# Cell builder of a graph network: PE's encode and transposes change places

## The reference

```python
# L1: a network that makes a 32x32 matrix for every edge, six message passes
eh  = relu(e_feat @ en1_w.T + en1_b)             # 200,000 x 128: built once, in the cell builder
w_e = (eh @ en2_w.T + en2_b).reshape(-1, D, D)
for _ in range(6):
    msg = einsum('ei,eio->eo', out[src], w_e)
    agg = segment_sum(msg, dst, num_segments=n_nodes) + conv_bias
    h   = gru_cell(relu(agg), h, ...)
# L0, L2, L3: out = segment_sum(weight[e] * x[src[e]], dst[e]), with different weights
```

## Time and profile before

| what | value |
|---|---|
| time, median of 3 runs | 24,022.46 us |
| lowest and highest run | 24,014.54 and 24,035.85 us |
| the profiled execution, its span | 30,532.6 us |
| the cell builder in it | 5,141 us, from 3,385 to 8,526 |
| DVE, POOL, PE, ACT busy in the cell builder | 3,460, 3,032, 2,962, 2,566 us |
| granted TensorE clock in the cell builder | 0.87 |

### The profile page before, as it was taken

The page is one execution under the profiler, slowest core; times in us unless marked ns, Lnnn a source line. Parts: engine busy times, 40 slices in busy tenths (PEclk is TensorE's granted clock), DMA queues, the critical chain, the costliest instruction groups (busy, mean ns, idle before and its releaser), DMA issues. The chain is left out here.

```text
span 30532.6 us, 420576 instructions
## 1 busy us (share of the span) xinstructions
PE 18622.1 (61%) x121575; PEld 13266.8 (43%) x121575; DVE 11720.7 (38%) x29589; ACT 7911.3 (26%) x20853; POOL 14020.9 (46%) x16639
## 2 busy tenths in 40 slices
PE   3333555555655676667666766676666766676654
PEld 3333322222244454455444554455445544554444
DVE  5444566666710333233323333233323332333220
ACT  0000344445510222222222322232222222232210
POOL 4886355555610444534453445344443445344520
PEclk5555788888977777777777877787777777787777
DMA  3222233322278222112211221122112221122147
GB/s 97 48 49 69 85 122 118 113 99 93 68 293 344 66 64 59 52 58 65 58 54 53 68 63 55 48 69 63 56 53 60 63 59 54 57 65 60 55 142 308
DMA packets 1398480, 2692.30 MB, mean 88 GB/s; under 512 B 938471, under 2 KB 1104704, under 8 KB 1189106
## 3 DMA queue, kind: packets, MB, share of 16 engines
q10 hardware_dynamic: 335568, 1445.71, 13.4%
q1 hardware_dynamic: 709952, 1053.68, 10.0%
q0 software_dynamic: 352256, 186.21, 4.3%
HBM read 2105.10 MB, written 1242.55 MB: 110 GB/s over the span
## 5 line engine op out<-in xcount | busy, mean ns | idle before, releaser
L785 POOL DMA_INDIRECT sb_xg<-node_rows,sb_src_c x9408 | 8876.9, 944 | 11917.8 <-SPq L803 6579.1
L921 PE MATMUL banks<-sb_work,sb_eh_sb 128*128 128x256 f32 x29184 | 8833.9, 453 | 1693.7 <-issue 1358.2
L921 PEld LDWEIGHTS banks<-sb_work,sb_eh_sb 128*128 128x128 f32 x29184 | 6472.3, 229 | 3674.0 <-issue 2259.6
L874 DVE TENSOR_TENSOR sb_work<-sb_xs,banks_p 128x2048 f32<-128x2048 f32 x1824 | 4171.1, 2288 | 9843.7 <-remote 5895.0
L978 ACT ACTIVATE sb_work<-banks 128x512 f32<-128x512 f32 x7296 | 4124.9, 599 | 11185.0 <-remote 7003.8
L1200 PE MATMUL banks<-sb_hot_code,sb_xs 128*128 128x392 bf16 x7296 | 1874.5, 371 | 2173.7 <-DVE sb_work L1163 1435.1
L1163 DVE SCALAR_TENSOR_TENSOR sb_work<-sb_work,sb_eh_sb,banks 128x784 f32 x2432 | 2502.3, 1029 | 572.4 <-PE banks L1202 484.1
L864 DVE COPY sb_xs<-sb_xg 128x32 f32 x14592 | 1762.7, 191 | 2459.9 <-issue 2268.6
L907 PE MATMUL banks_p<-sb_work,sb_en 128*32 128x256 f32 x29184 | 2084.7, 391 | 778.6 <-issue 766.1
L367 POOL DMA_INDIRECT slots<-sb_rows,sb_slot_u x1600 | 2108.6, 1318 | 786.7 <-issue 762.6
L1079 POOL TENSOR_SCALAR sb_xs<-sb_codes,sb_code 128x128 bf16<-128x128 f16 x2432 | 1516.6, 624 | 2067.3 <-PE banks L1202 2067.1
(11 more groups left out here) (281 smaller groups left out, 13084.1 us busy)
## 6 DMA issues: line engine op xcount, KB each, us to landing
sb_eh_sb<-eh ACTq DMA_DIRECT2D x912, 1024.0 KB
weights_between<-sb_work ACTq DMA_DIRECT2D x305, 1568.0 KB
edges_between<-sb_work ACTq DMA_DIRECT2D x305, 1568.0 KB
sb_work<-weights_between SPq DMA_DIRECT2D x147, 3136.0 KB, 12.5
sb_work<-edges_between SPq DMA_DIRECT2D x98, 3136.0 KB, 12.4
eh<-sb_eh_sb ACTq DMA_DIRECT2D x304, 512.0 KB, 2.6
sb_xg<-node_rows,sb_src_c POOLq DMA_INDIRECT x9408
sb_win_row<-window_rows SPq DMA_DIRECT2D x100, 488.3 KB
```

The source lines that it names most:

```text
L785: nc.gpsimd.indirect_dma_start(m.xg_ring[:, row % RING * D:(row % RING + 1) * D], None, m.node_dram, bass.IndirectOffsetOnAxis(ap=m.src_c[ ...
L874: V.tensor_tensor(m.spread[q], m.xs[h].rearrange("s (t i) -> s t i", i=D)[:, tiles, :].unsqueeze(3) .broadcast_to([P, TS, D, WN]), m.mask_ ...
L921: o = mm(m.ps_pair[u % 4][:, v, :, :], m.eh[h % 2][:, t * K:(t + 1) * K], m.spread[t // TS][:, t % TS, :, :], start=True, stop=True)
```

## The change

All in `build_cells`. In half c the engines now run:

- PE: tiles 0 and 1, encode of c, tiles 2 to 4, transposes of c+1, tiles 5 to 7.
- ACT: row operations of tiles 0 to 3, ReLU and DMA of c-1, tiles 4 and 5, copy of c+1, tiles 6 and 7, flush.
- DVE: adds 0 to 6, bias of c (its own half), add 7.

The first half's transposes and copy stand ahead of the loop, and on PE and ACT the last body is written out as well, since the last half has no successor to transpose.

```diff
+            keep_turned(0, 0, True)
+            for i, n, h in batches(act, behind=1):
                 for q in range(2):
                     c = n * 2 + q
-                    act.wait_ge(turned, c + 1)
-                    if not first(i, h):
-                        act.wait_ge(encoded, c - 1)
-                    nc.scalar.activation(m.attr_t[q], m.ps_turn[q], ACT.Copy).then_inc(turned_sb, 1)
                     for t in range(q * TS, q * TS + TS):
...
                         r.then_inc(weighted, 1)
+                        if t % TS == 3 and not (first(i, h) and q == 0):
+                            rectify(c - 1)
+                        if t % TS == 5 and not (isinstance(c, int) and c == last):
+                            keep_turned(c + 1, 1 - q, first(i, h) and q == 0)
                     if not (first(i, h) and q == 0):
-                        rectify(c - 1)
                         flush(i, c, 2 * h + q)
...
                     add(t)
-                    if t % TS == TS // 2 and not (first(i, h) and q == 0):
-                        bias(n * 2 + q - 1, first(i, h) and q == 1)
-            bias(2 * BATCHES - 1, False)
+                    if t % TS == 6:
+                        bias(n * 2 + q, first(i, h) and q == 0)
...
+                        if t % TS == 1:
+                            encode(c, q, first(i, h) and q == 0)
+                        if t % TS == 4 and not (isinstance(c, int) and c == last):
+                            turn_rows(c + 1, 1 - q, n + 1 + q, first(i, h) and q == 0)
```

More of the change, by code:

```diff
@@ L1030, in build_cells, with batches @@
         slots_v = m.slots.rearrange("(s t) r -> s t r", t=TP)
-        def batches(eng):
-            for i in peeled(eng, BODIES):
+        last = 2 * BATCHES - 1
+        def batches(eng, behind=0):
+            for i in peeled(eng, BODIES, behind=behind):
                 for h in range(L):
@@ L1101, in rectify, with keep_turned @@
                 act.dma_start(m.eh_dram[:, bass.ds(c * EC * K, EC * K)], m.eh_now).then_inc(eh_out, 16)
-            for i, n, h in batches(act):
+            def keep_turned(c, q, early):
+                act.wait_ge(turned, c + 1)
+                if not early:
+                    act.wait_ge(encoded, c - 1)
+                nc.scalar.activation(m.attr_t[q], m.ps_turn[q], ACT.Copy).then_inc(turned_sb, 1)
+            keep_turned(0, 0, True)
+            for i, n, h in batches(act, behind=1):
                 for q in range(2):
                     c = n * 2 + q
-                    act.wait_ge(turned, c + 1)
-                    if not first(i, h):
-                        act.wait_ge(encoded, c - 1)
-                    nc.scalar.activation(m.attr_t[q], m.ps_turn[q], ACT.Copy).then_inc(turned_sb, 1)
                     for t in range(q * TS, q * TS + TS):
@@ L1118, in _ @@
                         r.then_inc(weighted, 1)
+                        if t % TS == 3 and not (first(i, h) and q == 0):
+                            rectify(c - 1)
+                        if t % TS == 5 and not (isinstance(c, int) and c == last):
+                            keep_turned(c + 1, 1 - q, first(i, h) and q == 0)
                     if not (first(i, h) and q == 0):
-                        rectify(c - 1)
                         flush(i, c, 2 * h + q)
-            rectify(2 * BATCHES - 1)
+            rectify(last)
             flush(BODIES, 2 * BATCHES, 0)
@@ L1182, in _, with turn_rows, encode @@
             mm = nc.tensor.matmul
-            for i, n, h in batches(pe):
+            def turn_rows(c, q, loads, early):
+                pe.wait_ge(rows_in[q], loads * 16)
+                if not early:
+                    pe.wait_ge(turned_sb, c - 1)
+                for g in range(2):
+                    mt = nc.tensor.transpose(m.ps_turn[q][:, g * P:(g + 1) * P], m.attr[q][:, g * P:(g + 1) * P],
+                                             m.ident[:, :])
+                mt.then_inc(turned, 1)
+            def encode(c, q, early):
+                pe.wait_ge(turned_sb, c + 1)
+                if not early:
+                    pe.wait_ge(biased, c)
+                for g in range(2):
+                    me = mm(m.ps_encoded[:, g, :], m.attr_t[q][:, g * P:(g + 1) * P], m.en1[:, :], start=True, stop=True)
+                me.then_inc(encoded, 1)
+            turn_rows(0, 0, 1, True)
+            for i, n, h in batches(pe, behind=1):
                 for q in range(2):
                     c = n * 2 + q
[L1186 to L1192, removed]
                     for t in range(q * TS, q * TS + TS):
```

## The result

The changed kernel takes 23,474.44 us (median of 4 runs, 23,472.86 to 23,476.29), against 24,026.48 for the kernel before (4 runs): ratio 0.9772, 95% interval 0.9758 to 0.9786, 552 us less. The forecast was 23,780; the direction and the range held, the saving is 2.3 times the forecast's 240.

A forecast was written before the change was run, and what follows sets the result against it. A circle of waits (flush behind ReLU, ReLU behind bias, next rows behind flush) was taken to bound the cell builder. Periods over all halves summed to 4,879 us against 5,148, 269 saved, 240 timed: 23,780, range 23,430 to 24,050.

The forecast's parts named there:

- 18.6 + d: Forecast length in us of a half whose flush has data, from add 0 to the next add 0; before, 21.18.
- d: Delay of add 2 by the encode between PE's tiles 1 and 2: 1.7 us, between 0.74 and 3.5; 0.6 behind a flush.
- The conversion: Profile savings count 0.79 to 1 in timed runs, the profiled span being 27% longer: 269 us taken as 240.
- The circle of no-flush even halves: Add 2, transposes, copy, two tiles, flush step and next add 0 in series: 11.9 us plus d.
- Batch starts: Every second half DVE loads places into registers: 3.63 us from add 7 to next add 0, period 13.2 + d.
- The landing: Flush data may land 0 to 0.86 us sooner, as SP's row load goes earlier; 0.4 taken.
- first: Rival: clock stays high, d is 0.74 everywhere; 370 to 468 us saved, about 23,600; chance 0.28.
- second: Rival: no change, d near 3.0, the wait for the encode gives back the earlier flush's gain; 24,022; chance 0.13.
- fourth: Rival: PE at half clock before every half, tiles 0 to 2 and encode slow; 24,240, 190 to 240 slower; chance 0.14.
- third: Rival: flush-bound, only the 97 halves with flush data gain; 85 us saved, 23,950; chance 0.03.

The follow-up runs named there:

- the flush in series: The changed kernel, with ACT waiting for its own row operations of the half ahead of the flush's register load: 23,559.99 us, +86 against the change.

## Why the prediction was right or wrong

*The step that failed: the flush behind the copy, in the term 18.6 + d for flush halves.* It put the register load and the two issues, 2.62 + 0.26 as read behind the encoded rows' DMA, in series behind two tiles of row operations. Measured from the copy's start: 2.32 at the median (2.25 to 2.35) instead of 4.90. In the changed kernel ACT's sequencer starts the load 0.49 behind the start of the copy, while the engine works on the rows; the flush in series gave 1.6 of the 2.6 back. The load itself is 0.77, not 1.51, which is another 0.74. The copy came where the sum had it, 6.46 after S against 4.88 + 1.7. So the second flush DMA left 8.78 after S on average, not 9.76 + 1.7. Of these 2.7 us 0.4 were lost behind it, mostly at loop ends, where the half ends 11.8 behind that DMA. The 97 flush halves took 18.03 on average, not 20.3: 97 x 2.27 = 220 of the 283 us by which the saving of all halves (552) exceeds the 269.

*The conversion.* 0.79 to 1 took 29 us off. The surplus of the earlier trace rows was all behind the stage; the trace of one execution did not tell that, so the stage's own difference was the better estimate.

*d.* Where no flush stands ahead, 1.70 (odd) and 1.85 (even) against 1.7: right in the mean, in part by luck. With a slow encode it was 2.3 on average, not 3.5 (tile 2 is fast again), but 115 of these 205 halves had a slow encode, where 1.7 between ends of 0.74 and 3.5 stands for about a third. Behind a flush, 0.6: odd 0.13, but even 1.85. There the register load takes 3.7 us beside the flush, tile 0 comes late, and with the flush landing earlier no time is left to encode in.

*The circle of no-flush even halves.* 13.07 against a forecast mean of 13.08, by two errors: d larger behind a flush, and the circle through ACT 2.6 shorter, so that DVE's own adds set the pace (add 7 at 11.83 and 1.24 to S').

*Batch starts.* 3.63 forecast from add 7 to S', 2.91 measured: the load takes 1.12 where it took 1.56 at the median before, when the encoded rows' write had just been issued. That is most of 14.39 against 13.66 in odd halves. DVE was not busy there; it waited for its registers.

*The landing.* A gain of 0.4 was taken: from 9.57 and 9.21 (even, odd) to 9.06 and 8.72, 0.5. The row load's 0.13 MB no longer move between the second flush DMA and S', as forecast, but the write of the encoded rows is now issued there, 5.2 to 5.3 behind that DMA in these flush halves, where none stood before; the forecast had not seen it. The Trainium skill, "DMA: Bandwidth & Descriptors" (section "Queues, rings and completion order"), has each DMA engine take its queues in turn, packet by packet. The full 0.86 that was expected by it did not come, and which part of the 0.5 is the load's is not shown.

*Rivals.* The clock did not stay high (first), and its fall did not undo the gain (second and fourth). Flush-bound (third) had the right place, not the price: over half of the saving is there.

## What to carry to other kernels

Before a stall's length is used as a cost at a new place, ask which part of it is the engine and which its sequencer: here a register load and two DMA issues behind two tiles of queued row operations ran beside them, 1.6 us of each flush. Issue the transfer that is waited for first; here a swap of two lines gave more than moving five steps. A stretch of waiting is cover for what stands behind it, and whoever shortens it must price what it hid. And look at what fills PE's gaps before you place matmuls: here filler behind tile 7 cut the slow encodes from 59% to 14%, and the encode itself behind tile 7 left none. Before a wait is put down to the engine that was moved, ask which one ran without idle time in front of it: moving the ReLU three times could not shorten the even halves, which the encode on PE held.

## What the runs showed of the hardware

- A register load is not a constant. On ACT it took 1.51 us at the median right behind the issue of a 0.5 MB DMA (the kernel before), 0.72 with the flush put ahead of that DMA, and 0.77 beside row operations (after). On DVE it took 1.12 at the median after the change where no flush stood ahead, 1.56 in the order of before, and, behind a flush half, 3.3 to 3.7 at the median in the kernels whose flush of 3.2 MB was then in flight.
- Matmuls that nothing reads, 1.89 us a half, made the program 1.1% faster (23,474 to 23,218).
- One profiled execution was 27% longer than the timed runs, all of it in later stages whose clock was 0.76 instead of 0.86; the stage under study was true to the timed runs.
